# One pipeline of eleven steps behind six attention layers

## Time and profile before

| | us |
|---|---|
| median of 3 runs | 946.88 |
| lowest, highest | 946.32, 947.59 |
| profiled execution | 947.66 |
| its span, first to last instruction | 945.9 |
| PE busy | 816.8 |
| DVE busy | 703.6 |
| ACT busy | 598.7 |
| POOL busy | 424.9 |
| mean granted clock of TensorE | 0.927 |

### The profile page before, as it was taken

One profiled execution on the slowest core, in us unless ns is written; L12 is line 12 of the kernel. 1 busy time (PEld: TensorE's weight loads), 2 busy tenths in 40 slices (PEclk: granted clock), 3 DMA queues, 4 the chain that ended last, 5 costly groups with the idle time before them and its releaser, 6 DMA issues.

```text
span 945.9 us, 15397 instructions
## 1 busy us (share of the span) xinstructions
PE 816.8 (86%) x5085; PEld 689.2 (73%) x5092; DVE 703.6 (74%) x2019; ACT 598.7 (63%) x1275; POOL 424.9 (45%) x706
## 2 busy tenths in 40 slices
PE   2688999999999999999999999989878766888543
PEld 2577878888888888888888888889657643646432
DVE  5788888888888888888888887620456789689843
ACT  3366767777777777777777677531778751236554
POOL 4455435445544554445444644311366350253554
PEclk9599999999999999999999999985998998989866
DMA  9100001000000000000100000000000000000001
GB/s 262 52 1 1 1 1 34 2 1 1 25 11 1 1 11 25 1 1 1 35 1 2 1 1 1 1 1 0 1 1 1 1 1 0 0 2 12 23 12 45
DMA packets 19726, 13.65 MB, mean 14 GB/s; under 512 B 2488, under 2 KB 18495, under 8 KB 19647
## 3 DMA queue, kind: packets, MB, share of 16 engines
q1 hardware_dynamic: 19646, 12.67, 4.7%
HBM read 10.57 MB, written 2.10 MB: 13 GB/s over the span
## 4 chain that ended last, share of the span: by engine, by line
PE 65%; DVE 13%; ACT 9%; POOL 6%; issue 5%; DMA 0%; POOLq 0%; DVEq 0%; ACTq 0%
PE PS L358 58%; PE PS L368 7%; ACT XR L898 2%; POOL R L683 1%; ACT HL L982 1%; ACT XR L856 1%; ACT EK L856 1%; DVE ST L1098 1%; POOL RSTD L741 1%; DVE STATS L1191 1%; ACT HL L986 1%; DVE XI L1184 1%; POOL QB L757 1%; POOL RSTD L735 1%; POOL X L775 1%
## 5 line engine op out<-in xcount | busy, mean ns | idle before, releaser
L358 PE MATMUL PS<-W,HL 128*128 128x128 f32 x1536 | 201.7, 275 | 0.0
L358 PEld LDWEIGHTS PS<-W,HL 128*128 128x128 f32 x1536 | 193.4, 191 | 8.2
L919 ACT ACTIVATE HL<-PS 128x512 f32<-128x512 f32 x192 | 109.4, 594 | 22.7 <-PE PS L358 18.2
L724 POOL TENSOR_TENSOR JOIN<-STATS 128x8 f32<-128x8 f32 (+1 forms) x50 | 12.9, 257 | 220.5 <-DVE STATS L1191 220.5
L368 PE MATMUL PS<-ID,XR 128*128 128x128 f32 x448 | 73.2, 288 | 33.2 <-ACT XR L856 17.1
L358 PE MATMUL PS<-X2H,W1L 128*128 128x512 f32 x192 | 88.6, 461 | 5.9 <-issue 4.4
L368 PEld LDWEIGHTS PS<-ID,XR 128*128 128x128 f32 x448 | 53.0, 146 | 53.7 <-ACT XR L898 20.1
L939 ACT ACTIVATE EK<-PS,NKM 128x512 f32<-128x512 f32 x48 | 33.1, 689 | 88.1 <-DVE NKM L1261 88.1
L1191 DVE BATCH_NORM_STATS2 STATS<-XI 128x6 f32<-128x128 f32 x384 | 82.5, 278 | 0.3
L763 POOL TENSOR_TENSOR QB<-QB,QRC 128x512 f32<-128x512 f32 x48 | 51.0, 1062 | 69.6 <-DVE QRC L1295 69.6
L898 ACT ACTIVATE XR<-XI,RSTD 128x128 f32<-128x128 f32 x192 | 61.5, 393 | 29.9 <-POOL RSTD L741 29.6
(11 more groups left out here) (210 smaller groups left out, 2129.9 us busy)
## 6 DMA issues: line engine op xcount, KB each, us to landing
W<-in_w SPq DMA_DIRECT2D x12, 256.0 KB
X<-in_x SPq DMA_DIRECT2D x8, 256.0 KB, 4.9
out<-X SPq DMA_DIRECT2D x8, 256.0 KB, 2.3
QKV<-in_qkv SPq DMA_DIRECT2D x6, 192.0 KB, 2.9
FWD<-in_fwd SPq DMA_DIRECT2D x1, 1024.0 KB, 5.5
INV<-in_inv SPq DMA_DIRECT2D x1, 1024.0 KB, 8.4
WO<-in_wo SPq DMA_DIRECT2D x6, 64.0 KB
FWDX<-in_fwdx SPq DMA_DIRECT2D x1, 256.0 KB, 6.2
```

The lines of the kernel that those rows point to most:

```text
L358: return nc.tensor.matmul(o, l, r, start=start, stop=stop, skip_group_check=True)
L919: nc.scalar.activation(HL[f][:, :], pH[f % 2][:, :], ACT.Prelu, alpha=LEAK).then_inc(s["hl"], 1)
```

## The change

- **One pipeline.** The separate stages are gone. The 8 samples go on behind the 48 items: what was the first norm and addition of the spiking block happens in steps 48 to 55 with the layers' own statistics and powers (`join_next`, `ln1_power`, `second_scale`, `second_turn`), and its hidden and projection blocks are `h` and `y` of items 48 to 55. Eleven stages are numbered by how many steps behind 48 they stand: ADD, PART, TURN, FFN, SPIKE, STATE, CONV, BACK, SHIFT, GATE, FINISH. Steps 48 to 50 still are `step`, steps 51 to 65 are `late_step`, in which each engine has one list with all stages.
- **Convolution sample by sample.** `transform` makes the 16 products of 128 columns of one sample into two banks; `products` multiplies them on DVE as four operations and two sums; `inverse` and `back_bands` follow one step later.
- **Mixing folded into weights.** Wk and Wr are split once into mu times the weight and the rest; keys and gate are each a product with the sample plus a product with the sample shifted by one position, summed in PSUM. The three DVE operations per sample go.
- **Tables at the start.** The loads for the kernel table are issued by ACT instead of SP, ahead of its first work. `decay` and the 16 `exponents` go from DVE in steps 8 to 24 to POOL, before and in step 0; `powers` to ACT's steps 0 and 1; the 64 slices to PE's steps 1 to 3, the butterfly of k to step 6. Centring of weights and `spectrum` go into steps 42 to 46.
- Buffers: the late stages use slices of the table's space (BIG), which is free by then; statistics have five sets; waits inside DVE and POOL count one semaphore each (`part_done`).

The core of the diff:

```diff
-TABLES = BATCH
-CHUNKS = {TABLES + 1 + i: i for i in range(PAIRS // 4)}
-SLICES = {0: range(0, 36), 1: range(36, PAIRS)}
-STARTS = [0, 1, 2, 3, None, None, 4, 5, 6, 7]
+ADD, PART, TURN, FFN, SPIKE, STATE, CONV, BACK, SHIFT, GATE, FINISH = range(11)
+def sample(n, stage):
+    v = n - ITEMS - stage
+    return v if 0 <= v < BATCH else None
+def late(step):
+    for n in range(ITEMS + 3, ITEMS + BATCH + FINISH):
+        step(n)
+CHUNKS = {0: (range(0, 3), range(3, 7)), 1: (range(7, 12), range(12, 16))}
+SLICES = {1: ((0, 8), (8, 14), (14, 20)), 2: ((20, 28), (28, 36), (36, 44)), 3: ((44, 51), (51, 58), (58, 64))}
+SPECTRUM = {ITEMS - 4: (0, 1, 2, 3), ITEMS - 3: (4, 5, 6, 7), ITEMS - 2: (8,)}
...
 # TensorE, late steps
+            def late_step(n):
...
+                if conv is not None:
+                    project_in(conv, n)
+                if has_m:
+                    h(m, 2)
+                    y(m, 0)
+                if back is not None:
+                    inverse(back)
+                if has_m:
+                    y(m, 1)
+                    h(m, 3)
+                if gate is not None:
+                    key_and_gate(gate, n)
+                if has_m:
+                    y(m, 2)
+                if has_x:
+                    second_turn(n)
+                if has_m:
+                    y(m, 3)
+                if spike is not None:
+                    count(spike, n)
+                if conv is not None:
+                    transform(conv, n)
+                if gate is not None:
+                    value(gate)
+                if back is not None:
+                    project_out(back, n)
+                if state is not None:
+                    state_turn(state, n)
+                if has_x:
+                    h(m + 1, 0)
+                if shift is not None:
+                    shift_turn(shift, n)
+                if has_x:
+                    h(m + 1, 1)
+            def key_and_gate(v, n):
...
+                mm(pXT[:, :], WK1[:, :], SH[:, 1:1 + SEQ], True, False)
+                mm(pXT[:, :], WK2[:, :], SH[:, 0:SEQ], False, True).then_inc(s["k2_ps"], 1)
...
+                for j in range(TILES):
+                    mm(pQ[:, j * P:(j + 1) * P], SH[:, 1 + j * P:1 + (j + 1) * P], WR1[:, :], True, False)
+                    last = mm(pQ[:, j * P:(j + 1) * P], SH[:, j * P:(j + 1) * P], WR2[:, :], False, True)
...
 # GpSimd, before step 0
+            decay()
+            exponents(0)
             input_rstd(0)
+            exponents(1)
+            exponents(2)
             join(0, TILES, 0)
             ln1_power(0)
             input_rstd(1)
             input_rstd(2)
+            for p4 in range(3, 7):
+                exponents(p4)
...
 # GpSimd, step
-                if has_next:
-                    ln1_power(n + 1)
+                ln1_power(n + 1)
+                if n == 0:
+                    for p4 in range(7, 9):
+                        exponents(p4)
...
+                if n == 0:
+                    for p4 in range(9, PAIRS // 4):
+                        exponents(p4)
```

More of the change, by code:

```diff
@@ L1 @@
+import itertools
 import numpy as np
@@ L395, in step, with slices @@
                 m = n - 3
[L397 to L408, removed]
[L410 to L422 removed]
+                def slices(place):
+                    if n in SLICES:
+                        kernel_slices(*SLICES[n][place])
                 if has_n:
@@ new lines, in transform @@
+            def transform(v, n):
+                pe.wait_ge(s["bands"], v + 1)
+                pe.wait_ge(s["kf"], 3)
+                if passed(n, BACK):
+                    pe.wait_ge(s["back"], passed(n, BACK))
+                for half, bank in enumerate((pK, pW)):
+                    for k in range(TILES):
+                        for j in range(2):
+                            last = mm(bank[:, k * P:(k + 1) * P], FWD[:, j * BINS * P + half * SEQ + k * P:][:, 0:P],
+                                      V[:, (2 * k + j) * P:(2 * k + j + 1) * P], j == 0, j == 1)
+                    last.then_inc(s["f_ps"], 1)
@@ new lines, in value, with count @@
+            def value(v):
+                pe.wait_ge(s["r_sq"], v + 1)
+                for j in range(TILES):
+                    last = mm(pXT[:, j * P:(j + 1) * P], SQ[:, j * P:(j + 1) * P], WVT[:, :])
+                last.then_inc(s["v_ps"], 1)
+            def count(v, n):
+                if passed(n - 1, SPIKE):
+                    pe.wait_ge(s["cnt_z"], passed(n - 1, SPIKE))
+                if passed(n, GATE):
+                    pe.wait_ge(s["r_sig"], passed(n, GATE))
+                for t in range(STEPS):
+                    pe.wait_ge(s["spk"], v * STEPS + t + 1)
+                    last = mm(pQ[:, :], IDB[:, :], SPK[t][:, :], t == 0, t == STEPS - 1)
+                last.then_inc(s["cnt_ps"], 1)
@@ L1491, in _, with bands, spikes @@
-            slots(slot)
+            def bands(v):
+                dve.wait_ge(s["u_ps"], v + 1)
+                tt(tiles(U[:, :]), tiles(pXT[:, :]), BIN[:, :].unsqueeze(1).broadcast_to([P, TILES, P]),
+                   ALU.add).then_inc(s["u_sum"], 1)
+                dve.wait_ge(s["u_sum"], v + 1)
+                if some(v):
+                    dve.wait_ge(s["f_ps"], 2 * v)
+                butterfly(U, V).then_inc(s["bands"], 1)
+            def spikes(v):
+                dve.wait_ge(s["ym"], v + 1)
+                if some(v):
+                    dve.wait_ge(s["cnt_ps"], v)
+                for t in range(STEPS):
+                    ts(SPK[t][:, :], YM[:, :], LEVELS[t], None, ALU.is_gt).then_inc(s["spk"], 1)
```

1233 lines of the change are left out of this document (544 added, 689 removed).

## The result

| | kernel before | changed kernel |
|---|---|---|
| median, us | 946.91 (945.75 to 949.09, 16 runs) | 935.82 (932.63 to 944.70, 16 runs) |
| ratio | | 0.9893, 95% interval 0.9874 to 0.9913 |
| profiled execution, us (span) | 947.66 (945.9) | 935.99 (934.1) |

The change makes the kernel 11.1 us faster; 928 was forecast, 7.8 less than measured, and 935.82 lies in the range of 885 to 955. The profiled execution of the changed kernel is a typical one. In the two traces the time behind the layers fell from 341.2 us (604.7 to 945.9) to 299.6 (634.5 to 934.1), 41.6 less, of which the block of small products alone was 27.0. The start and the layers took 29.8 us more. The gain is the small rest of two large numbers.

A forecast was written before the change was run, and what follows sets the result against it. PE bounds the layers; after 627.1 us, chains between engines, stage ends and a lowered clock do. 626.7 (step 47's end) + 27 + 274 = 927.7, with 1.8 and less 0.8 called 928; range 885 to 955.

The forecast's parts named there:

- Start: Steps 0 to 3: table work in front adds +6 to first scaling, +5 by step 2, +3 for slices; together 14.
- Butterfly, +2: Step 6: the table's butterfly on DVE adds 2 us.
- Layers, +6: In the layers: centring and table products on full PE add 5.2 us, with one wait 6.
- Steps 48 to 50, 27: Steps 48 to 50: transposes, two hidden blocks and ACT's XR scaling raise 22.4 us to 27.
- Late steps, 274: Steps 51 to 65: queues followed in order sum to 260.3 us; with clock and port prices, 274.
- the two prices: Late steps: 8 us for clock drops (bounds 0 and 34) and 6 for port meetings (3 to 12).
- Port meetings: Late butterflies: six more DVE operations slowed beside POOL ones, 1.23 us instead of 0.68; 3 to 12, 6 taken.
- The loop over the relus: Late steps: next relus stand behind ZOUT and ZCNT on ACT, and PE's whole step waits for them.
- Folding: Gate samples: mixing folded into weights adds 1.75 us of PE a sample and removes three DVE operations, 1.9 us.
- The full-engine case (879): Rival: waits overlap, each late step takes its fullest engine, DVE or PE; 49 less, 879 us; chance 0.24.
- The falling clock (960): Rival: PE's idle in late steps pulls the clock to 0.72, start's slices at lower level; 960 us; chance 0.17.
- The lock on the port: Rival: exponents blocks, POOL adds and powers hold DVE at full price; some 18 more, 946 us; chance 0.06.

The follow-up runs named there:

- relu_first: Changed kernel with the next item's first two relu-and-square pairs issued on ScalarE at the end of each late step, ahead of the output normalisation: 930.28 us.
- no_slices: Changed kernel with the kernel table's 128 eight-column matmuls replaced by one product (wrong output, only time read): 931.04 us, one execution.
- butterfly_spread: Changed kernel with the table butterfly's ten VectorE operations moved from the head of step 6 to six pieces in steps 16 to 21: 932.27 us.
- no_powers: Changed kernel with ScalarE's sixteen table exponentials left out (wrong table values, only time read): 938.17 us, one execution.

## Why the prediction was right, and where not

The direction, the mechanism and the size of the late part held. The sum failed by 6.4 us of span: the start was 8.4 us longer than its term, the other terms together 2.0 shorter. And folding was priced too low.

- **Start.** The first scaling was put at 17.3 us and came at 17.42; step 2's was to be 12 us behind the old 41 and came at 53.03 (the old one is at 40.02, so 13.0 behind). The next term failed: "I put +3 on the path" for the slices, "so most falls into gaps". The start grew by 6.7 us between steps 2 and 4 (+13.0 to +19.7), by 9.3 in the trace of relu_first, and no_slices gives 6.1 at step 4 and 7.8 at step 7. From 56 to 75 us PE was busy 18.54 of 19 us and had no gaps for them, and it ran part of them at the lower level, as the row at 55.27 us shows.
- **Butterfly, +2.** 5.7 us (17.4 against 11.7); butterfly_spread shows it. The stop itself is 2.8 of them, near the term; the 2.9 us at the lower level of the clock were not counted, and not every execution has them. With 2.0 us more by step 2 than the terms give and 1.4 regained between steps 7 and 42, these two make the start 24.4 us (step 42) instead of 16.
- **Its own sign.** A start more than 20 us behind was to make the prediction wrong. The start came 25.8 us behind at step 7 and 24.4 at step 42. By this sign its account of the start is wrong, though the time lies in the range. That no block of slices would run at the lower level was another sign, and it failed too.
- **Layers, +6.** 5.4 (+24.4 at step 42, +29.8 at 47). **Steps 48 to 50, 27:** 26.6.
- **Late steps, 274:** 273.0 from the first hidden block of step 51 (661.1 us) to the end. Step by step, by the starts of h(m,2): 8.9 (9), 14.2 (14.6), 16.1 (15.2), 16.5 (15.7), 22.3 (22), 24.8 (22.7), 27.2 (27.1). The clock was 0.90 and 0.88 there, as the 0.89 taken. These differences are 3.6 us over the terms before the two prices, the rest of the late steps 9.1 over; 14 had been put on them together. Port meetings: five VectorE operations were 1.0 to 1.1 us longer than others of their form, 5.0 us, for the 6 taken. (The rule of the Trainium skill, SBUF — State Buffer, "SBUF: two separate sides", bears on this price, which was the second of the two, and not the first.) One of them, and POOL's operation beside it:

```profile
795.92 1.26 POOL L767 TENSOR_TENSOR X<-X,EK 128x512 f32<-128x512 f32 x1
796.05 1.28 DVE L1163 TENSOR_TENSOR BIG<-EKT,FLY 128x128 f32<-128x128 f32 x1
```

- **The loop over the relus** was named rightly as what ends last, but it was taken for the bound. Of its 19.9 us of waits 5.5 were worth anything. That VectorE "stands idle behind x2h, `count` and `value`" stood beside it without the question why: because PE runs the 3.7 us transform first. That order cost 19 us.
- **Folding** was priced at +1.75 us for PE and 1.9 us less for VectorE per sample. The operations taken off stand at the head of the loop through VectorE, and unfolded they meet POOL in six of eight steps: 11 us for eight samples, a part of it by the clock.
- **Rivals.** The full-engine case (879) did not come about, but for a reason that can be edited: with the orders of PE's, ACT's, POOL's and VectorE's lists changed and the table late the same kernel takes 897. Its sign did not appear: VectorE was busy 92.1 of the 123.2 us from 716.8 to 840 us, 75% and not 90. It had been given 0.24. The falling clock (960) did not either, with 0.88 to 0.90 in the late part; it did fall in steps 2, 3 and 6. One reason given for it misreads: the clock was lowest, 0.57, in the stretch in which PE was busy 28.25 of 30.1 us, and not in the one with the most idle time (0.81). The lock on the port has the size of the prediction in the changed kernel, and shows a higher price once folding is undone.

## What to carry to other kernels

A wait that ends last gives only the difference to the next loop: before pricing it, follow each other engine's queue through the same step, and ask of every wait which instruction stands in front of the producer on its engine. In an in-order pipeline, put what another engine waits for ahead of long products that nobody needs yet. Work that comes off one place should not be put in the start, where the engines depend on each other, but spread in pieces over steps whose order hides it: here even PE's full steps were cheaper (10.8 us for the small products) than the start. And before a difference between two single traces is put down to an edit, look for a trace with the same instructions there.

## What was not expected of the hardware

- One idle stretch of 2.7 us of PE, amid full ones at full clock, was followed by 5.7 us at a granted clock of 0.50. The same idle stretch, behind the same instructions, was followed by full clock in the traces of relu_first and no_powers, and by 3 to 7 us at the lower level in four others.
- With the same instructions, the clock from 56 to 75 us was 0.65 in one trace and 0.50 in another, and the next step began 2.7 us later. From 38 to 41.5 us the record even says full clock beside products of the length that they have at the lower level.
- The changed kernel's 16 runs spread over 12.1 us, with the mean granted clock at 0.940 in the longest and 0.961 in the shortest; the kernel before spread over 3.3 us. Why was not tested.
